# A selective scan with Softplus in batches, plane sums on TensorE and u read straight

## The reference

```
xz = x @ Win;  xb, z = split(xz)                    # 256 channels each
xb = silu(depthwise3x3(xb) + conv_b)                # u
xs = four orders of u: rows, rows reversed, columns, columns reversed
dt, B, C = split(xs @ Wxproj)                       # 8, 1, 1 rows for each order
delta = softplus(dt_weight[k] @ dt + dt_bias[k])
for each step t:  s = exp(delta * A) * s + delta * u * B;   y = C * s
y = y0 + y1 + y2 + y3 (each put back in row order) + D * u
yz = y * silu(z);   out = layernorm(yz) @ Wout
```

## Time and profile before

| | us |
|---|---|
| median of 3 runs (4608.92 to 4612.55) | 4612.47 |
| the profiled execution: its own time | 4611.34 |
| its span, first to last instruction | 4609.5 |
| convolution, scan, tail, last stage begin at about | 3167, 3639, 4396, 4427 |

### The profile page before, as it was taken

The page is one execution under the profiler, slowest core; times in us unless marked ns, Lnnn a source line. Parts: engine busy times, 40 slices in busy tenths (PEclk is TensorE's granted clock), DMA queues, the critical chain, the costliest instruction groups (busy, mean ns, idle before and its releaser), DMA issues. The chain is left out here.

```text
span 4609.5 us, 73934 instructions
## 1 busy us (share of the span) xinstructions
PE 3873.8 (84%) x25590; PEld 2996.1 (65%) x25590; DVE 3406.9 (74%) x7889; ACT 2678.2 (58%) x6018; POOL 1391.3 (30%) x1373
## 2 busy tenths in 40 slices
PE   6888887799999999999999999676999644455579
PEld 4666665699988998899888998444666311111148
DVE  4666666577787777777787777695666798899934
ACT  3666665577776777767776667333222466666621
POOL 2434443100010000200010000112244599999910
PEclk9999999799999999999999999898999755555579
DMA  7777774200010000100010000212222311122143
GB/s 205 204 199 198 197 198 137 76 24 21 18 37 27 20 24 16 42 24 24 17 39 13 10 10 10 67 62 95 77 77 71 145 55 55 60 69 71 58 151 102
DMA packets 274687, 346.40 MB, mean 75 GB/s; under 512 B 34954, under 2 KB 159754, under 8 KB 272778
## 3 DMA queue, kind: packets, MB, share of 16 engines
q1 hardware_dynamic: 261738, 320.55, 22.8%
q0 software_dynamic: 12288, 16.92, 1.4%
q10 hardware_dynamic: 288, 4.19, 0.2%
HBM read 209.58 MB, written 130.02 MB: 74 GB/s over the span
## 5 line engine op out<-in xcount | busy, mean ns | idle before, releaser
L864 ACT ACTIVATE l_ph<-l_T 128x512 fp32r<-128x512 f32 x1024 | 612.4, 598 | 547.2 <-PE l_T L777 547.2
L974 DVE TENSOR_TENSOR l_pl<-l_T,l_ph 128x512 fp32r<-128x512 f32 x1024 | 707.3, 691 | 274.9 <-ACT l_ph L864 274.2
L963 DVE CUSTOM_DVE_ANT_0 l_pr<-l_S,l_zero 128x512 f32<-128x512 f32 x1024 | 704.7, 689 | 74.1 <-PE l_S L700 11.2
L869 ACT ACTIVATE l_pr<-l_pr,l_st 128x512 f32<-128x512 f32 x1024 | 731.5, 714 | 1.1 <-DVE l_st L969 1.0
L789 PE MATMUL l_O<-l_ph,l_vh 128*128 128x256 f32 x2048 | 661.7, 323 | 12.2 <-DVE l_pl L974 12.1
L777 PE MATMUL l_T<-l_ident,l_pr 128*128 128x128 f32 x4096 | 612.8, 272 | 0.0
L777 PEld LDWEIGHTS l_T<-l_ident,l_pr 128*128 128x128 f32 x4096 | 507.6, 140 | 136.2
L790 PE MATMUL l_O<-l_ph,l_vl 128*128 128x256 f32 x2048 | 577.9, 282 | 0.0
L791 PE MATMUL l_O<-l_pl,l_vh 128*128 128x256 f32 x2048 | 576.8, 282 | 0.0
L1005 POOL TENSOR_TENSOR l_xs<-l_xs,l_bob 128x128 f32<-128x128 f32 x128 | 57.1, 461 | 1644.7 <-DMA l_xs<-x 1643.6
L1658 PE MATMUL l3b_C<-l_D,l_sel 32*128 32x512 f32 x256 | 216.4, 845 | 384.5 <-DVE l3b_E L1716 384.1
(11 more groups left out here) (241 smaller groups left out, 8842.7 us busy)
## 6 DMA issues: line engine op xcount, KB each, us to landing
hls<-l_hl SPq DMA_DIRECT2D x64, 512.0 KB, 4.7
l_qs<-hls SPq DMA_DIRECT2D x96, 256.0 KB, 3.8
l_ks<-hls SPq DMA_DIRECT2D x96, 256.0 KB, 4.0
l_xc<-x1t SPq DMA_DIRECT2D x64, 256.0 KB, 2.7
zs<-l3a_tmp SPq DMA_DIRECT2D x64, 256.0 KB, 2.0
l3b_z<-zs SPq DMA_DIRECT2D x64, 256.0 KB, 2.8
yz<-l3b_z SPq DMA_DIRECT2D x64, 256.0 KB, 2.0
l3c_y<-yz SPq DMA_DIRECT2D x16, 1024.0 KB, 17.1
```

The source lines that it names most:

```text
L864: e.activation(ph[:, i, :], psT[:, i, :], ACT.Copy).then_inc(p_hi, 1)
L869: e.activation(pr[:, s, es], pr[:, s, es], ACT.Exp, bias=st[:, s, 9:10], scale=SC, accum_out=st[:, s, 10 + k:11 + k]).then_inc(exped, 1)
L963: e.tensor_tensor_reduce(pr[:, s, ks], psS[:, bk, :], zero[:].broadcast_to([128, 512]), 1.0, -3.0e38, ALU.add, ALU.max, st[:, s, kc:kc + 1 ...
L974: e.tensor_tensor(pl[:, i, :], psT[:, i, :], f32(ph[:, i, :]), ALU.subtract).then_inc(p_lo, 1)
```

## The change

- `U0` (four images of half 0) gives way to `planes`, 2 x 2 planes of 4096 tokens. u times B, both halves, is stored in DRAM in row order (`ub[0]`, L1368) and, by a copy on ScalarE into a plane in column order, also in column order (`ub[1]`, two stores of 2 MB for each image on SP's queue).
- The scan reads u in contiguous tiles of 1024 tokens from DRAM, four buffers.
- Softplus is one ACTIVATE, six units in a row, then six Exp; two PSUM banks for its input, four for the decay.
- The product by C is written for even a4 into plane 0 or 1 (rows, columns) directly, for odd a4 into a ring of three, and GpSimd adds only these, reversed, to the plane.
- A gate sums the two planes and `acc` by three accumulating matmuls in a bank that it shares with C; gates stand at steps T with T % 6 of 1 or 5. z has four buffers.
- The skip sums stay in `acc`; their copy in DRAM is gone.

```diff
-        self.U0 = tile("u0", [128, NI, TOK])
+        self.planes = tile("planes", [128, 2, 2, TOK])
...
+            def store_turned(b):
+                w.wait_ge(turned_u, 16 * b + 16)
+                for h in range(2):
+                    e.dma_start(ub[1, h, b], planes[:, b % 2, h, :]).then_inc(K.turned_out[b % 2], 16)
...
-                    e.dma_start(ub1[bb, :, 512 * c0:512 * c0 + 512], U1[:, (g - 2) % 3, :]).then_inc(u_out[(g - 2) % 3], 16)
+                    e.dma_start(ub[0, :, bb, :, 512 * c0:512 * c0 + 512].rearrange("h p t -> p h t"), U[:, :, (g - 2) % 3, :]).then_inc(u_out[(g - 2) % 3], 16)
+                    if g >= 3 and (g - 3) % 8 == 7:
+                        store_turned((g - 3) // 8)
...
+            for g in range(N + 3):
+                if g >= 3:
+                    b, ch = divmod(g - 3, 8)
+                    for h in range(2):
+                        w.wait_ge(times_B, 2 * (g - 3) + h + 1)
+                        if b >= 2:
+                            w.wait_ge(K.turned_out[b % 2], 32 * (b // 2))
+                        o = planes[:, b % 2, h, :].rearrange("p (w h) -> p w h", h=64)[:, :, 8 * ch:8 * ch + 8]
+                        e.activation(o, u_of(g - 3, h).rearrange("p (r c) -> p c r", c=64), ACT.Copy).then_inc(turned_u, 1)
...
+        tT, tU, tE, tZ = P.sb("dt", [128, 2 * B, 512]), P.sb("du", [128, 3, 512]), P.sb("E", [128, 3, 512]), P.sb("z", [128, 4, 512])
+        U = P.sb("u", [128, 4, 1024])
+        psd = P.ps("d", [128, 2, 512])
+        psL = P.ps("L", [128, 4, 512])
...
+        gates = {}
         for k in range(2 * NI):
+            slots = [T for T in range(32 * k + 36, M) if T % B in (1, 5)][:8]
             for c in range(8):
-                fetches[32 * k + 35 + 2 * c] = k, c
-                gates[32 * k + 37 + 2 * c] = k, c
-        times = range(M + 24)
+                gates[slots[c] if len(slots) == 8 else M + 3 + c] = 8 * k + c
+        times = range(-1, M + 13)
+
+        def deltas(T):
+
+            if T < 0:
+                return range(B)
+            b, r = divmod(T, B)
+            m = B * b + B
+            return [x for x in {1: (m, m + 1), 2: (m + 2,), 3: (m + 3, m + 4, m + 5)}.get(r, ()) if x < M]
+
+
+        use, order = {}, []
+        for T in times:
+            if T + 1 < M:
+                order.append(("C", T + 1))
+            if T in gates:
+                order.append(("X", gates[T]))
+        use = {what: i for i, what in enumerate(order)}
...
+            def claim(what):
+                i = use[what]
+                if i >= 2:
+                    last, x = order[i - 2]
+                    w.wait_ge(c_done if last == "C" else gated, x + 1)
+                return psC[:, i % 2, :]
+
+            for T in times:
+                if T + 1 < M:
+                    n, h, a4, c = unit(T + 1)
+                    rows = slice(32 * a4, 32 * a4 + 32)
+                    e.matmul(claim(("C", T + 1)), sel[rows, 1, :], part(D[rows, :], n, c), start=True, stop=True).then_inc(C_full, 1)
+                for m in deltas(T):
+                    n, h, a4, c = unit(m)
+                    rows = slice(32 * n, 32 * n + 32)
+                    if m >= 2:
+                        w.wait_ge(soft, m - 1)
+                    e.matmul(psd[:, m % 2, :], dtw[rows, 256 * a4 + 128 * h:256 * a4 + 128 * h + 128], part(D[rows, :], a4, c), start=True, stop=True).then_inc(d_full, 1)
                 if T in gates:
+                    k, c = divmod(gates[T], 8)
                     w.wait_ge(ident_in, 16)
+                    w.wait_ge(c_done, 32 * k + 32)
+                    w.wait_ge(added, 16 * k + 16)
+                    X = claim(("X", gates[T]))
+                    e.matmul(X, ident[:], part(planes[:, k % 2, 0, :], 0, c), start=True, stop=False)
+                    e.matmul(X, ident[:], part(planes[:, k % 2, 1, :], 2, c), start=False, stop=False)
+                    e.matmul(X, ident[:], part(acc[:, k % 2, :], k // 2, c), start=False, stop=True).then_inc(X_full, 1)
...
+            for b in range(0, M, B):
+                batch = range(b, min(b + B, M))
+                for m in batch:
+                    w.wait_ge(d_full, m + 1)
+                    if m >= 2 * B:
+                        w.wait_ge(dued, m - 2 * B + 1)
+                    e.activation(tT[:, m % (2 * B), :], psd[:, m % 2, :], ACT.Softplus).then_inc(soft, 1)
+                for m in batch:
                     n, h, a4, c = unit(m)
                     w.wait_ge(soft, m + 1)
+                    if m >= 4:
+                        w.wait_ge(scanned, m - 3)
+                    e.activation(psL[:, m % 4, :], tT[:, m % (2 * B), :], ACT.Exp, scale=cA[:, 2 * a4 + h:2 * a4 + h + 1]).then_inc(decayed, 1)
...
+                if 0 <= T < M:
+                    n, h, a4, c = unit(T)
+                    k = 2 * n + h
+                    G = tU[:, T % 3, :]
+                    w.wait_ge(dued, T + 1)
+                    w.wait_ge(decayed, T + 1)
                     if c:
+                        w.wait_ge(scanned, T)
+                    e.tensor_tensor_scan(G, psL[:, T % 4, :], G, tU[:, (T - 1) % 3, 511:512] if c else 0.0, ALU.mult, ALU.add).then_inc(scanned, 1)
+                    if a4 % 2:
+                        E = tE[:, odd(T) % 3, :]
+                        if odd(T) >= 3:
+                            w.wait_ge(added, odd(T) - 2)
+                    else:
+                        E = part(planes[:, k % 2, a4 // 2, :], 0, c)
+                        if k == 1:
+                            w.wait_ge(K.turned_out[1], 64)
+                        elif k:
+                            w.wait_ge(X_full, 8 * (k - 1))
+                    w.wait_ge(scanned, T + 1)
+                    w.wait_ge(C_full, T + 1)
+                    e.tensor_tensor(E, psC[:, use["C", T] % 2, :], G, ALU.mult).then_inc(c_done, 1)
+                if T - 1 in gates:
+                    j = gates[T - 1]
+                    w.wait_ge(z_in[j % 4], 16 * (j // 4 + 1))
                     w.wait_ge(X_full, j + 1)
+                    e.tensor_tensor(tZ[:, j % 4, :], psC[:, use["X", j] % 2, :], tZ[:, j % 4, :], ALU.mult).then_inc(gated, 1)
...
+                m = T + 1
+                if m < M:
                     n, h, a4, c = unit(m)
                     w.wait_ge(soft, m + 1)
+                    w.wait_ge(u_in[m // 2 % 4], 16 * (m // 8 + 1))
                     if m >= 3:
                         w.wait_ge(scanned, m - 1)
                         w.wait_ge(c_done, m - 2)
+                    s = m // 2 % 4
+                    u = U[:, s, 1023 - 512 * (c % 2):511 - 512 * (c % 2) if c % 2 == 0 else None:-1] if n % 2 else U[:, s, 512 * (c % 2):512 * (c % 2) + 512]
+                    e.tensor_tensor(tU[:, m % 3, :], tT[:, m % (2 * B), :], u, ALU.mult).then_inc(dued, 1)
+                m = T - 1
+                if 0 <= m < M and unit(m)[2] % 2:
+                    n, h, a4, c = unit(m)
+                    k = 2 * n + h
+                    o = part(planes[:, k % 2, a4 // 2, :], 1, c)
+                    w.wait_ge(c_done, m + 1)
+                    e.tensor_tensor(o, o, tE[:, odd(m) % 3, :], ALU.add).then_inc(added, 1)
...
```

More of the change, by code:

```diff
@@ L1452, in scalar @@
             w.wait_ge(cleared, 1)
-            for g in range(N + 1):
+            for g in range(N + 3):
[7 more added lines that the diff above has]
+                        e.activation(o, u_of(g - 3, h).rearrange("p (r c) -> p c r", c=64), ACT.Copy).then_inc(turned_u, 1)
                 if g < N:
@@ L1646, in sync, with load, fetch @@
-            for i in range(2):
-                w.wait_ge(y_out[i], 16 * 8 * NI)
+            def load(p):
+                n, h, a4, c = unit(2 * p)
+                c0 = 6 - c if n % 2 else c
+                if p >= 4:
+                    w.wait_ge(dued, 2 * p - 6)
+                if n == 2:
+                    w.wait_ge(K.turned_out[1], 64)
+                e.dma_start(U[:, p % 4, :], ub[n // 2, h, a4, :, 512 * c0:512 * c0 + 1024]).then_inc(u_in[p % 4], 16)
+            def fetch(j):
+                k, c = divmod(j, 8)
+                if j >= 4:
+                    w.wait_ge(y_out[j % 4], 16 * (j // 4))
+                e.dma_start(tZ[:, j % 4, :], zs[k // 2, k % 2, :, 512 * c:512 * c + 512]).then_inc(z_in[j % 4], 16)
@@ new lines, in sync @@
+            for p in range(4):
+                load(p)
+            for j in range(3):
+                fetch(j)
+            for T in times:
+                if T >= 0 and T % 2 == 0 and T // 2 + 4 < M // 2:
+                    load(T // 2 + 4)
+                if T - 2 in gates:
+                    j = gates[T - 2]
+                    k, c = divmod(j, 8)
+                    w.wait_ge(gated, j + 1)
+                    e.dma_start(yz[k // 2, k % 2, :, 512 * c:512 * c + 512], tZ[:, j % 4, :]).then_inc(y_out[j % 4], 16)
+                    if j + 3 < 16 * NI:
+                        fetch(j + 3)
@@ L1983, in program @@
         K = Carried(nc, ctx)
```

(4 more changed lines are left out.)

153 lines of the change are left out of this document (32 added, 121 removed).

## The result

| | before | after |
|---|---|---|
| median (4 runs each, same chip) | 4611.16 (4608.92 to 4612.55) | 4669.69 (4663.90 to 4679.23) |
| the profiled execution: its own time, its span | 4611.34, 4609.5 | 4679.23, 4677.5 |

The account below looks back on a forecast made before the run. TensorE was taken to bound the convolution, VectorE and GpSimd together the scan. 4611.3 + 17 (copies) + 23 (stores) + 4 (scan start) - 19.5 (first units) - 45 (gated units) - 3 (tail) = 4588 us, range 4510 to 4655.

Parts of the forecast that it names:

- First 32 units: Ungated start of the scan: VectorE loses the min/max, 1.92 us a unit; 67.5 instead of 87.0, 19.5 us saved.
- The gates: Scan's 224 units: three sums a gate, 4.40 us at half clock, 1.75 at full; 615 instead of 660, 45 saved.
- The clock in the gates: TensorE's clock rises late in a triple; 16 of 56 gates find it high, 40 cost 3.92 us each.
- The tail: Last product to last gate's end: one triple at 4.7, seven at 2.56; 25.8 instead of 29.1 us, 3 saved.
- Copies: Convolution: ScalarE's turned copies, 0.6 us each, lengthen the loop in 21 groups by 0.8: 17 us lost (0 to 38).
- Stores: Convolution: 2 MB stores ahead of x on SP's queue; 4.2 MB take 9.7 us, two stalls of 11.5: 23 lost.
- Start of the scan: First u tile lands behind the last 4.2 MB of stores on the queue; first product 4 us late (0 to 7).
- Table loads: ScalarE in the scan: two loads per six units, 1.28 us each with no drain beside; 1 us charged ungated.
- The sum: Whole kernel: 4611.3 + 17 + 23 + 4 - 19.5 - 45 - 3 = 4588 us.
- Rivals: Other outcomes: clock never up 4667 (0.20), clock always up 4501 (0.13), convolution free 4548 (0.19), dear table switch 4645 (0.06).
- clock never up: Scan stays at half clock: each gate costs 4.40 us, the tail 18 more; 4667, slower; chance 0.20.
- point of decision: Scan gates: the never-rising clock decides from a mean gate cost of 4.4 down to about 3.7 us, where gain is gone.

Follow-up runs that it names:

- e2: The changed kernel with only the first of a gate's three sums (second plane and skip sum left out): 4493.1 us, ratio 0.9743 to before.
- e1: The changed kernel with the second and third sums of a gate read straight instead of turned or reversed: 4645.4 us, ratio 1.0069 to before.
- e3: The changed kernel with ScalarE's two turned copies one group earlier, before the rounding of x: 4647.2 us, ratio 1.0072 to before.
- e4: The changed kernel with the 2 MB stores issued from ScalarE's queue instead of SP's, once the copies are done: 4664.5 us, ratio 1.0110.
- e10: The changed kernel with both convolution edits, copies one group earlier and 2 MB stores on ScalarE's queue: 4625.7 us, ratio 1.0026 to before.

## Why the prediction was wrong, point by point

- **First 32 units (-19.5 forecast, -19.5 measured).** Right, down to its parts: even units 1.9 apart, GpSimd's deficit in odd ones softened by its lead.
- **The gates (the step that failed; 615 forecast for 224 units, 663.2 measured).** Forecast were 430 for the units, 34 for the gates' own work and 151 of stall. Measured were 185.7 of stall and, with the same 34, 443 for the units; e2 gives nearly the same, 448 (498.2 - 34 - 15.8). So 35 of the 48 us are stall, and 13 are units at 1.98 instead of 1.92: 5 of them are waits of the scan for GpSimd's product and for the Exp, the cause of the rest no run isolates. The price of a triple at half clock (3.79 of stall) was exact. Wrong was "at full clock 0.05 + 2.56": it took the 0.86 of a straight operand for operands that are read turned. At full clock a triple is 0.86 + 1.71 + 0.86 for k < 4 and 0.86 + 1.71 + 1.71 from k = 4 on. e1 takes just that away: 29 of the 35. From first sum to gate after has 4.98 us in the mean where one operand is turned and 5.49 where two are, e1 4.65 and 4.70.
- **The clock in the gates.** That it would rise late in most triples was right, and the mean of 0.66 lies in the forecast's 0.5 to 0.8. That 16 of 56 would find it high was not: with no operand turned (e1) 3 took under 4.2 us. By the forecast's durations the mean from first sum to gate would have been 4.49, and e1 has 4.68; in the time of e1 that is the last 6 us of stall (634.2 - 34 - 443 = 157, against 151).
- **The tail (-3 forecast, +9.4 measured).** The same step: seven triples at 4.29 instead of 2.56 are 12.1 of the 12.4.
- **Copies (17 forecast, 32 measured).** For the greater part the term's size: 0.6 was taken, the low end of 0.6 to 1.0, and even the high end was under the 1.12 that it is. A pair stands 2.2 us in the loop instead of 1.2. e3 gives 25 back by place alone; where the other 7 come from stays open. That they hide in the last image was nearly right (2.6 us lost there).
- **Stores (23 forecast, 31 measured).** The mechanism and its first term were right: 12.0 us from issue to landing where 9.7 plus landing was forecast, 10.5 and 10.1 lost in the two groups. Left out was the group behind, which lost 5 more each time. Since in e4 and e10 the stores also leave earlier, no run tells the order of the queue from the DMA engines' being full; for the next term one does.
- **Start of the scan (+4 forecast, +8.1 measured).** The first u tile lands after the last 4.2 MB, as said, only later. That this is one queue's order, as the forecast had it, is not so: in e10, with two queues, it lands as late. The row of after for GpSimd's first product shows that wait:

```profile
3718.91 3.71 POOL L1792 TENSOR_TENSOR l3b_du<-l3b_dt,l3b_u 128x512 f32<-128x512 f32 x3 [22.35 <-DMA l3b_u<-ub]
```

- **Table loads.** Right: 1.28 each and no loss beside it; ScalarE waits for others all through. The 2.66 of the Trainium skill ("ScalarE: Activation LUTs", What ACT_TABLE_LOAD costs) is not seen in these rows.
- **The sum.** The misses are 48 (gates), 12 (tail) and 30 (convolution and start), 90 in all, from -23.5 to +67. The runs tie 29 + 12 of them to the turned operand on TensorE (e1). On ScalarE it is the copy's 1.12 for 0.6, about 1 us more for a pair in each of 21 groups; that is worked out, and no run isolates it. For GpSimd the forecast had seen the same effect in the earlier trace rows.
- **Rivals.** None was the case. The one that came nearest in time (4667, clock never up) is wrong in its mechanism: the clock does rise. That it came near is luck, of three misses that add up. Its point of decision, 3.7 us a gate, was passed all the same: with the units' 13 put on the gates they came to (663.2 - 430) / 56 = 4.16.

## What to carry to other kernels

An operand's duration is that of its access pattern: before a row's duration is used for a new instruction, compare the step between elements, and where the row is of a straight one, put the turned one at about twice its time (here 1.71 against 0.86 on TensorE at full clock, 1.12 against 0.60 on ScalarE). When work moves to another engine, add up that engine's load at the clock that it has there before the waits: a wait that can be hidden and a load that can't look the same in the view of waits. And a large store is issued as soon as its data is there, and where no load that an engine waits for follows within its 12 us; another queue does not help a load that meets it, as the start of the scan shows.

## What was not expected of the hardware

- An fp32 matmul of 128x512 whose moving operand steps 256 bytes takes 1.71 us at either level of the clock; a straight one 0.86 at full and 1.71 at half. The Trainium skill ("SBUF — State Buffer", Door 1: The DMA port swizzle) says that each access which crosses to a new 16-byte line pays; the direction agrees at full clock, at half clock nothing of it shows, and it gives no duration.
- An ACTIVATE Copy of 128x512 with a turned source, written in runs of eight elements, takes 1117 ns, Softplus of that size, read straight, 599.
- A scan with both inputs in SBUF takes 2.10 us beside GpSimd's products and 1.27 with one of them in PSUM, and slows GpSimd from 1.33 to 1.91 at the same time. With both in SBUF and GpSimd idle it takes 1.27 again.
- A load issued on one queue while 4.2 MB leave on another waits as long as behind them on the same queue: 12.9 and 13.2 us for the first u tile of the scan.
